# Attention outputs and gates with time on the partitions, turned in steps five and six, weight splits in other stretches of GpSimd

## What is computed

```
for each head (32 value heads, two to a key head), each time t:
    S  = S * exp(g_t)
    S  = S + k_t * (v_t - k_t S) * beta_t
    o_t = q_t S
xn    = o * rsqrt(mean(o^2) + eps) * norm_w        # over the 128 columns of a head
gated = silu(z) * xn                                # z = x W_z
y     = x + gated W_out
```

## Time and profile before

| what | us |
|---|---|
| median of 3 runs | 3989.26 |
| lowest and highest | 3987.52, 3992.92 |
| the profiled execution, its own time | 3988.65 |
| its span, first to last instruction | 3986.9 |
| attention, 62 periods of a unit | 3108.08 |

### The profile page before, as it was taken

How to read it: one execution, slowest core, us unless ns; L and a number is a source line. 1 busy time by engine, 2 the same in 40 slices (tenths; PEclk the granted TensorE clock), 3 DMA queues, 4 the chain that set the end, 5 groups by cost and what they waited for, 6 DMA issues and landing times. The chain is left out here.

```text
span 3986.9 us, 74528 instructions
## 1 busy us (share of the span) xinstructions
PE 3711.7 (93%) x28324; PEld 2984.8 (75%) x28324; DVE 2447.1 (61%) x4347; ACT 1986.3 (50%) x4272; POOL 2344.9 (59%) x2805
## 2 busy tenths in 40 slices
PE   5995699999999999999999999999999999998798
PEld 4884477777777777777777777777777777776587
DVE  4654366666666666666666666666666666664464
ACT  3432355555555555555555555555555555553243
POOL 2102567676766666676676767676767676763110
PEclk8997799999999999999999999999999999998899
DMA  4333100000000000000000000000000000001521
GB/s 165 97 33 67 50 22 23 23 23 22 23 22 23 22 23 22 23 22 23 22 23 22 23 23 23 22 23 22 23 22 23 19 22 22 25 16 36 175 54 33
DMA packets 142384, 140.32 MB, mean 35 GB/s; under 512 B 84176, under 2 KB 115152, under 8 KB 140880
## 3 DMA queue, kind: packets, MB, share of 16 engines
q1 hardware_dynamic: 136992, 120.16, 10.6%
q0 software_dynamic: 4464, 14.36, 1.0%
q10 hardware_dynamic: 576, 1.03, 0.1%
HBM read 109.11 MB, written 26.21 MB: 34 GB/s over the span
## 5 line engine op out<-in xcount | busy, mean ns | idle before, releaser
L1850 ACT ACTIVATE at_t<-at_inv 128x512 f16<-128x512 f32 x768 | 459.0, 598 | 783.0 <-PE at_inv L1659 783.0
L1458 PE MATMUL at_proj<-x_hi,at_w_hi 128*128 128x512 f32 x1536 | 669.4, 436 | 15.7 <-POOL at_w_lo L2103 15.7
L1458 PE MATMUL at_proj<-x_lo,at_w_hi 128*128 128x512 f32 x1536 | 663.4, 432 | 0.0
L1458 PE MATMUL at_proj<-x_hi,at_w_lo 128*128 128x512 f32 x1536 | 651.9, 424 | 0.0
L2033 DVE TENSOR_TENSOR at_pm<-at_prod,at_cst 128x512 f16<-128x512 f32 x768 | 529.6, 690 | 158.3 <-PE at_prod L1458 143.7
L2007 DVE SCALAR_TENSOR_TENSOR resid<-at_misc,at_fr,resid 128x512 f32<-128x512 f32 x512 | 383.3, 749 | 137.3 <-PE at_misc L1458 134.1
L1458 PE MATMUL at_prod<-at_t,at_nlhi 128*128 128x128 f16 x3584 | 377.5, 223 | 0.9 <-DVE at_pm L2040 0.9
L1657 PEld LDWEIGHTS at_inv<-at_pm,at_t 128*128 128x128 f16 x3072 | 214.0, 101 | 218.7 <-DVE at_pm L2033 139.0
L1458 PEld LDWEIGHTS at_proj<-x_hi,at_w_hi 128*128 128x128 f32 x1536 | 299.5, 195 | 55.3 <-issue 15.9
L1458 PEld LDWEIGHTS at_proj<-x_hi,at_w_lo 128*128 128x128 f32 x1536 | 301.8, 196 | 43.1
L1458 PEld LDWEIGHTS at_proj<-x_lo,at_w_hi 128*128 128x128 f32 x1536 | 303.6, 198 | 34.0
(11 more groups left out here) (282 smaller groups left out, 9512.3 us busy)
## 6 DMA issues: line engine op xcount, KB each, us to landing
at_gb<-decays SPq DMA_DIRECT2D x64, 512.0 KB, 3.7
at_e<-w_qkvz SPq DMA_DIRECT2D x32, 512.0 KB, 3.7
ffn_weights<-ffn_w SPq DMA_DIRECT2D x1, 11776.0 KB, 36.8
ffn_w<-ffn_weights POOLq DMA_DIRECT2D x4, 2688.0 KB, 23.5
at_gb<-w_qkvz SPq DMA_DIRECT2D x16, 512.0 KB, 3.6
at_gb<-w_out SPq DMA_DIRECT2D x16, 512.0 KB, 3.5
f_xnext<-x_in SPq DMA_DIRECT2D x4, 1024.0 KB, 5.2
f_xres<-x_res SPq DMA_DIRECT2D x4, 1024.0 KB, 5.2
```

The source lines that it names most:

```text
L1458: return nc.tensor.matmul(out, lhsT, rhs, start=start, stop=stop)
L1850: own["a_t"].up(A(grown(t16[:, s % R].rearrange("p a t -> p (a t)"), s // R), grown(psT[s % R], s // R), ACT.Copy))
```

## The change

**TensorE.** The output matmuls swap their operands, so that `psO` has time on the partitions. The gates are projected with time on the partitions too: `gate_part` has x stationary and both heads' gate weights moving, 48 matmuls of 256 columns in the place of 24 of 512, in steps 3 to 7, 9 to 11 and 12. `out_sums` goes. `turn_gated(h)` turns the finished gated outputs by four transposes into `psM` in step 5 (head 0) and 6 (head 1). `out_product(c)` sums both heads in one bank: 4 products of six matmuls, in steps 8 to 11. One more query matmul (8 in the place of 7) stands at the end of the slot, the other four in step 2.

**ScalarE.** `squares` works in chunks with a running sum (`accum_out`), which gives the sums of squares for each token. `gated(h)` reads the turned bank, scales by `nw` and writes `gt_hi`, in steps 5 and 6.

**VectorE.** `d_gate` has two inputs. `low(h)` computes `gt_lo` from the turned bank, `nw` and `gt_hi`, in steps 5 and 6. `out_add` is a plain add, 4 times, in steps 8 to 11. The three key taps that stood at the end of a slot are split: one there, one after `d_gate`, one in step 2.

**GpSimd.** `out_scale` takes the sums from ScalarE; `scale_gated(h)` multiplies the gated outputs by `fr`. `silu(K_U)` comes ahead of `kg`. `split_wo` and the third weight part are done in two halves, the first ahead of the key sums.

The core of the diff:

```diff
 
-                def out_product(i, of):
-
-                    h, c = i // CH, i % CH
+                def gate_part(u, first, end):
+
+                    if first == 0:
+                        if j % B == 0:
+                            wait(pe, "p_z", j // B + 1)
+                        bank_free(u, j)
+                    for k in range(first, end):
+                        c, hb = k // (3 * HB), k % (3 * HB) // 3
+                        tok = j % B * S + (2 * (u - Z0_U) + c) * P
+                        w, xs = ((w_hi, x_hi), (w_hi, x_lo), (w_lo, x_hi))[k % 3]
+                        last = mm(unit_bank[u][:, c * R * D:(c + 1) * R * D], xs[:, hb, tok:tok + P], w[:, hb, 4 * D:6 * D],
+                                  k % (3 * HB) == 0, k % (3 * HB) == 3 * HB - 1)
+                    if end == 6 * HB:
+                        own["s_z"].up(last)
+
+                def turn_gated(h, of):
+
                     wait(pe, "p_gt", R * of + h + 1)
-                    if of % B == 0:
+                    if h == 0:
+                        wait(pe, "d_aqk", R * (j + 1))
+                    else:
+                        wait(pe, "d_lo", R * of + h)
+                    for c in range(CH):
+                        last = nc.tensor.transpose(ch(psM, c), gated_of(h)[:, c, :], ident)
+                    own["s_gtr"].up(last)
+
+                def out_product(c, of):
+
+                    if of % B == 0 and c == 0:
                         wait(pe, "p_wo", R * (of // B + 1))
-                    if i > 0:
-                        wait(pe, "d_y", WPROD * of + i)
+                    if c > 0:
+                        wait(pe, "d_y", WPROD * of + c)
                     else:
-                        wait(pe, "d_aqk", R * (j + 1))
+                        wait(pe, "d_lo", R * (of + 1))
                     out = out_bank[:]
-                    mm(out, ch(gt_hi[:, h], c), wo_hi[:, h, :], True, False)
-                    mm(out, ch(gt_hi[:, h], c), wo_lo[:, h, :], False, False)
-                    own["s_w"].up(mm(out, ch(gt_lo[:, h], c), wo_hi[:, h, :], False, True))
+                    for h in range(R):
+                        mm(out, ch(gt_hi[:, h], c), wo_hi[:, h, :], h == 0, False)
+                        mm(out, ch(gt_hi[:, h], c), wo_lo[:, h, :], False, False)
+                        last = mm(out, ch(gt_lo[:, h], c), wo_hi[:, h, :], False, h == R - 1)
+                    own["s_w"].up(last)
 
                 def sums():
 
...
-                def out_sums(of):
-
-                    wait(pe, "a_sqo", R * (of + 1))
-                    if of == UNITS - 1:
-                        wait(pe, "d_z", 2 * UNITS)
-                    else:
-                        wait(pe, "d_conv", 4 * j + 1 if has_prep else 4 * j - 1)
-                    for i in range(R * CH):
-                        last = mm(psA[0][:, i:i + 1], ch(osq[:, i // CH], i % CH), ones[:, 0:1])
-                    own["s_sso"].up(last)
-
                 def level_0(i, g):
 
...
+                def gates_in(u, first, end):
+                    return lambda: gate_part(u, first, end)
+
+                if has_prep:
+                    fill[2].append(parts(Q_U, 8, 12))
+                if has_delta:
+                    fill[3].append(gates_in(Z0_U, 0, 6))
+                    fill[4].append(gates_in(Z0_U, 6, 16))
+                    fill[5].append(gates_in(Z0_U, 16, 20))
+                    fill[6].append(gates_in(Z0_U, 20, 24))
+                    fill[7].append(gates_in(Z1_U, 0, 10))
+                    for s in range(3):
+                        fill[9 + s].append(gates_in(Z1_U, 10 + 3 * s, 13 + 3 * s))
                 if behind:
-                    fill[2].append(lambda: out_sums(j - 1))
+                    for h in range(R):
+                        fill[5 + h].append(lambda h=h: turn_gated(h, j - 1))
+                    for c in range(WPROD):
+                        fill[8 + c].append(lambda c=c: out_product(c, j - 1))
+                if has_delta:
+                    fill[12].append(gates_in(Z1_U, 19, 24))
                 if has_prep:
-                    fill[3].append(parts(Q_U, 7, 12))
-                if has_delta:
-                    fill[4].append(parts(Z0_U, 0, 5))
-                    fill[5].append(parts(Z0_U, 5, 6))
-                    fill[6].append(parts(Z0_U, 7, 8))
-                    fill[7].append(parts(Z0_U, 9, 10))
-                    for k in range(5):
-                        fill[8 + k].append(parts(Z1_U, 2 * k, 2 * k + 1))
-                if behind:
-                    for i in range(WPROD):
-                        fill[5 + i].append(lambda i=i: out_product(i, j - 1))
-                if has_delta:
-                    fill[5].append(parts(Z0_U, 6, 7))
...
+                    fill[12].append(turn_k)
+                    fill[13].append(parts(V0_U, 0, 3))
+                    fill[14].append(parts(V0_U, 3, 6))
...
                             for h in range(R):
-                                mm(ch(psO[h], c), state[:, h, :], ch(qg[:, h], c - 1), True, False)
...
-                            last = mm(ch(psO[h], c), delta[:, h, :], ch(aqk[:, h], c), c == 0, True)
+                            last = mm(ch(psO[h], c), ch(aqk[:, h], c), delta[:, h, :], c == 0, True)
...
                     wait(act, "s_o", j + 1)
+                    wait(act, "p_fr", j)
                     if h < R - 1:
                         wait(act, "d_gate", R * j + h + 1)
-                    own["a_sqo"].up(A(osq[:, h, :], psO[h], ACT.Square))
+                    for c in range(CH):
+                        last = A(osq[:, h, c * P:(c + 1) * P], ch(psO[h], c), ACT.Square, scale=2 * D ** -0.5, accum_out=sso[:, h, c:c + 1])
+                    own["a_sqo"].up(last)
 
                 def gated(of, h):
                     wait(act, "s_w", WPROD * of)
-                    wait(act, "d_gate", R * of + h + 1)
-                    own["a_gt"].up(A(gt_hi[:, h, :], cv_z[:, h, :], ACT.Copy))
+                    wait(act, "s_gtr", R * of + h + 1)
+                    own["a_gt"].up(A(gt_hi[:, h, :], out_bank[:], ACT.Copy, scale=nw[:, 0:1]))
 
                 steps = {s: [] for s in range(R, STEPS + 1)}
                 if has_prep and not has_delta:
                     steps[2].append(lambda: tap(K_U))
+                if has_prep:
+                    steps[2].append(lambda: tap(Q_U))
+                    steps[3].append(lambda: tanh(K_U))
                 if behind:
-                    steps[2].append(lambda: gated(j - 1, 1))
+                    for h in range(R):
+                        steps[5 + h].append(lambda h=h: gated(j - 1, h))
                 if has_prep:
-                    steps[3].append(lambda: tap(Q_U))
-                    steps[4].append(lambda: tanh(K_U))
                     steps[7].append(lambda: tanh(Q_U))
                 if has_delta:
...
+
+                    wait(dve, "a_gt", R * of + h + 1)
+                    wait(dve, "s_dg", R * j if has_prep else R * (j - 1))
+                    own["d_lo"].up(V.scalar_tensor_tensor(gt_lo[:, h, :], out_bank[:], nw[:, 0:1], gt_hi[:, h, :], ALU.mult, ALU.subtract))
+
+                def out_add(c, of):
+
+                    wait(dve, "s_w", WPROD * of + c + 1)
                     row = resid[:, of % B * CH + c, :]
...
 
                 steps = {s: [] for s in range(STEPS)}
...
                     steps[3].append(lambda: qk(1))
                 if has_prep:
                     if not has_delta:
                         steps[3].append(lambda: conv(K_U, (1, 2, 3)))
-                    steps[4].append(lambda: conv(Q_U, (1,)))
+                if has_prep:
+                    steps[3].append(lambda: conv(Q_U, (1,)))
+                    steps[4].append(lambda: conv(Q_U, (2, 3)))
                 if behind:
-                    for i in range(WPROD):
-                        steps[5 + i].append(lambda i=i: out_add(i, j - 1))
-                if has_prep:
-                    for i in range(2):
-                        steps[5 + i].append(lambda i=i: conv(Q_U, (i + 2,)))
+                    for h in range(R):
+                        steps[5 + h].append(lambda h=h: low(h, j - 1))
+                    for c in range(WPROD):
+                        steps[8 + c].append(lambda c=c: out_add(c, j - 1))
                 if has_delta:
-                    steps[10].append(lambda: silu_z(Z0_U))
...
-                            conv(K_U, (1, 2, 3), j + 1)
+                            conv(K_U, (1,), j + 1)
                 if has_delta:
                     for h in range(R):
                         if h == 0:
                             wait(dve, "s_o", j + 1)
                         else:
                             wait(dve, "a_sqo", R * j + h)
-                        own["d_gate"].up(V.scalar_tensor_tensor(cv_z[:, h, :], psO[h], nw[:, 0:1], cv_z[:, h, :], ALU.mult, ALU.mult))
```

(32 more changed lines are left out.)

98 lines of the change are left out of this document (46 added, 52 removed).

## The result

| kernel | us, median | lowest to highest | ratio to before, 95% interval |
|---|---|---|---|
| before | 3988.39 | 3985.2 to 3992.92 | |
| after | 4096.26 | 4094.6 to 4099.63 | 1.0271, 1.0253 to 1.0288 |

A forecast was written before the change was run, and what follows sets the result against it. TensorE, busy 93% of the span, was taken as the bound, at 50.13 us a unit. The terms summed to +3.20, a unit of 51.87: +1.74 times 63 = +110 us, forecast 4100, range 4000 to 4170.

The forecast's parts named there:

- End of unit: Squares take 2.0 us instead of 1.0, but VectorE's first gating starts earlier; TensorE's start after the squares doesn't move.
- Step 2: `out_sums` goes (1.76 us), four query matmuls come (1.02); T(2), the start of step 2's inversion products, comes 0.76 us earlier.
- Steps 2 to 5: Nine VectorE operations of 0.65 us from step 2's mask to step 5's set the pace: +0.84 us a unit.
- the rival at 0.23: 256-column gate matmuls cost 0.23 us, not 0.12: about 1.9 us a unit more, 4220 us; chance 0.05.
- Steps 5 to 7: ScalarE's copy and high part, then VectorE's low part and mask, in a row: 3.05 us a step, +1.88.
- Steps 7 to 11: First output product +0.23 us; then each waits for the add before it in one bank, 2.51 a step, +1.80.
- Step 12 to the turn: Until the normed keys' turn: one product less, value matmuls earlier, shorter wait for ScalarE's scaling; 7.49 us against 8.28, -0.79.
- Sum of the clean unit: All step terms for a unit without clock falls or GpSimd waits: +3.20 us, giving 51.87 us.
- Falls and waits: Mean minus clean unit, 1.46 us: 0.5 TensorE waits for GpSimd's masked gates, 0.96 clock falls of 1.60 each; all go.
- the clock falls elsewhere: TensorE's clock halves in steps 6 and 7 instead; at 1.60 us in each unit 4200 us; chance 0.20.
- GpSimd: Output scaling replaces low parts, 2.6 us each; split halves fit 6.02 us of idle before the key sums; gate-mask waits go.
- The faster rival: Steps 5 to 7 and the output products hide as today: 48.19 us a unit, 3867 us; chance 0.13.

The follow-up runs named there:

- e11: Kernel after with ScalarE's high parts one step earlier, head 1's low part behind step 7's mask, one query tap moved to step 6: 3942.08 us, ratio 0.9868.
- e1: Kernel after with ScalarE's high part of each head placed ahead of its copy, one step earlier: 3968.75 us, ratio 0.9935.
- e3: Kernel after with GpSimd's weight splits whole and late again, as in the kernel before: 4106.52 us, ratio 1.0282.
- e5: Kernel before with GpSimd's two weight splits halved, one half ahead of the key sums: 3941.44 us, ratio 0.988.
- e10: Kernel before with both weight splits halved and the sixteen one-column matmuls in two runs of eight: 3966.68 us, ratio 0.9948.
- e7: Kernel after with ScalarE's high parts one step earlier and nine gate matmuls moved from steps 9 to 11 into 6 and 7: 4015.18 us, ratio 1.0065.
- e6: Kernel before with its sixteen one-column matmuls split in two runs of eight, the second in step 3: 3941.79 us, ratio 0.988.

## Why the prediction was right, by its steps

- **End of unit**: nothing was to move. The start after the squares is 2.70 us after the last output matmul's start (2069.24) against 2.65, with an idle of 0.45 us for the 0.63 of the earlier trace rows. Right.
- **Step 2**: -0.76 predicted; T(2) moved by -0.69, of which 0.05 is the line above.
- **Steps 2 to 5**: 5.87 us against 5.05, +0.82 for +0.84. That VectorE's nine operations set it was right (e11).
- **Gate matmuls** of 256 columns: 0.12 us, as taken; the rival at 0.23 fell.
- **Steps 5 to 7**: 3.07 and 3.06 for 3.05 each, +1.90 for +1.88. The chain of three engines was read rightly, and e1 shows that it is the core: 125 us.
- **Steps 7 to 11**: 1.92, then 2.45 a step. The term of the ring was mis-sized: 2.51 each, +1.80 for the three; measured 7.34, +1.61. From the add's end to the next product it is 0.05 us (2090.87 to 2090.92), not 0.15; the six matmuls take 1.27 and not 1.23.
- **Step 12 to the turn**: 7.46 us, -0.82 for -0.79.
- **Sum of the clean unit**: +3.05 for +3.20, 9 us of the time.
- **Falls and waits**: said to go wholly, 1.46 us a unit. They went but for 0.10: 11 falls are left. The price of 1.60 us compared two kinds of unit; between units of one kind it is 1.55. The rival "the clock falls elsewhere" had the place right, step 6, and the frequency and price wrong: one unit in five or six, 0.4 us each. The slow stretch lies in steps where TensorE waits for VectorE, which fits the lower price. These 6 us and the 9 above nearly cancel; the hit by 4 us is luck beyond some 10 us.
- **GpSimd**: the scaling of the outputs was taken as 2.6 us for both heads and took 2.04. The 0.5 us a unit were put to the halves alone; in the change they are worth 0.2 (e3), and GpSimd's larger lead fits the rest of the wait, though no run varied it alone. On the kernel before the halves gave 47 us, falls included (e5). But the prediction's 6.02 us of idle before the key sums is from a unit of another kind, and one with a fall: in the kind of unit where the gate weights are split GpSimd had 0.94 us, and one kind in four lost by the halves. In the change the same place has 4.9 us of idle without them (e3), so there the argument held.

The step that I would now work harder on is none of the sum: it is that a single place in ScalarE's order carried all of the loss. The faster rival asked for a T(5) to T(6) of under 2.2 us and called it impossible with three engines in a row; it was 1.79 as soon as the high part stood ahead of the copy.

## What to carry to other kernels

When an operation is put between the links of a ring, ask on each engine in what order it stands to the ring's own operation: here one place earlier on ScalarE and one later on VectorE were worth 171 us, with the same work. Compare units of the same kind, since a mean can hide one in four that loses (e5). Price idle time of TensorE with the clock that it may cost behind it (e10), and less where what comes next waits for another engine (after). And test edits together: one that is free under a wait costs its full length when the wait is gone (e7), and two that both live from the same slack of GpSimd can undo each other (e10).

## What the runs showed of the hardware

- A fall of the clock has no price of its own: a stretch of 3.4 us at 0.50 cost 1.55 us where TensorE had matmuls in a row (before) and 0.4 us where it waited for VectorE (after).
- Sixteen one-column matmuls in a row behind 0.63 us of idle brought the fall in 36 periods of 62; the same sixteen as eight and eight, the second run in the next step behind three matmuls of 512 columns, in none (e6).
- A multiplication on GpSimd with one factor repeated along the row took 1.02 us for 128x512, a plain one of two tiles 1.29 (after):

```profile
2074.57 2.04 POOL L2155 TENSOR_TENSOR at_cv_z<-at_cv_z,at_fr 128x512 f32<-128x512 f32 x2
2076.56 1.29 POOL L2161 TENSOR_TENSOR at_th<-at_th,at_cv_v 128x512 f32<-128x512 f32 x1
```
